# Lightning attention and quantised FFN block: wider DRAM rows for q and k, the first unit's q from fp32 products, another order in the mixed slots

## The reference

```
h    = layernorm(x)
q,k,v = split(h @ w_qkv.T + b_qkv)                # 16 heads of 32
per chunk of 128 tokens, per head, state S (32 x 32), decays lam:
  out = (q * decay_q) @ S + ((q @ k.T) * dmask) @ v
  S   = lam**128 * S + (k * decay_k).T @ v
x    = x + layernorm(out @ w_out.T + b_out)
g    = silu(layernorm(x) @ e4m3(gate_w) * gate_scale)
u    = layernorm(x) @ e4m3(up_w) * up_scale
x    = x + layernorm((g * u) @ e4m3(down_w) * down_scale)
```

## Time and profile before

| | before |
|---|---|
| runs | 988.04 us (987.9 to 988.89, 3 runs) |
| profiled execution | 988.57 us, span 986.8 us |
| TensorE busy | 958.7 us, 97% |
| VectorE busy | 690.4 us, 70% |
| ScalarE busy | 509.1 us, 52% |
| GpSimd busy | 687.6 us, 70% |
| main DMA queue | 296672 packets, 157.86 MB, 67.4% of 16 engines' span |
| DMA packets in all | 297642, of them 141632 under 512 B, 272832 under 2 KB |

### The profile page before, as it was taken

The page is one execution under the profiler, slowest core; times in us unless marked ns, Lnnn a source line. Parts: engine busy times, 40 slices in busy tenths (PEclk is TensorE's granted clock), DMA queues, the critical chain, the costliest instruction groups (busy, mean ns, idle before and its releaser), DMA issues.

```text
span 986.8 us, 22045 instructions
## 1 busy us (share of the span) xinstructions
PE 958.7 (97%) x8498; PEld 708.9 (72%) x8498; DVE 690.4 (70%) x1359; ACT 509.1 (52%) x985; POOL 687.6 (70%) x837
## 2 busy tenths in 40 slices
PE   8999999999998999999999999999999999999996
PEld 6777777786766777767677676767767676776764
DVE  7999998875887675767667576766757676665422
ACT  3656665565654544636354463635446363544522
POOL 2699998986775675849567584947758594775733
PEclk9999999999999999999999999999999999999999
DMA  9899899999983983847658284766828476512200
GB/s 322 210 290 265 255 276 293 277 254 297 229 207 88 202 180 56 196 93 163 131 127 176 61 194 94 163 128 129 191 48 193 92 165 125 127 52 43 41 26 22
DMA packets 297642, 159.88 MB, mean 162 GB/s; under 512 B 141632, under 2 KB 272832, under 8 KB 297408
## 3 DMA queue, kind: packets, MB, share of 16 engines
q1 hardware_dynamic: 296672, 157.86, 67.4%
q10 hardware_dynamic: 864, 0.61, 0.2%
HBM read 82.93 MB, written 41.94 MB: 127 GB/s over the span
## 4 chain that ended last, share of the span: by engine, by line
PE 57%; DVE 17%; POOL 11%; issue 10%; ACT 4%; DMA 1%; POOLq 0%; DVEq 0%; SPq 0%; ACTq 0%
PE bank L892 17%; PE bank L874 12%; PE bank L767 8%; PE att L767 7%; PE bank L782 7%; POOL att_pool L1059 4%; DVE stats L1326 3%; DVE p L1367 3%; DVE state_hl L1397 3%; DVE w_pool L1460 2%; POOL rstd L998 2%; ACT w_pool L596 2%; POOL w_pool L1077 2%; PE att L851 1%; DVE state L1386 1%
## 5 line engine op out<-in xcount | busy, mean ns | idle before, releaser
L874 PE MATMUL bank<-f_pool,gate_q 128*128 128x256 f16 x1536 | 185.0, 274 | 4.3 <-ACT w_pool L596 3.8
L874 PE MATMUL bank<-f_pool,up_q 128*128 128x256 f16 x1536 | 183.7, 273 | 1.5
L892 PE MATMUL bank<-down_q,w_pool 128*128 128x512 f16 x768 | 168.3, 379 | 0.0
L874 PEld LDWEIGHTS bank<-f_pool,gate_q 128*128 128x128 f16 x1536 | 147.4, 98 | 27.0 <-ACT w_pool L596 6.5
L874 PEld LDWEIGHTS bank<-f_pool,up_q 128*128 128x128 f16 x1536 | 149.4, 98 | 22.4 <-DVE w_pool L1460 5.1
L1059 POOL TENSOR_TENSOR att_pool<-p,att_pool 128x512 f16<-128x512 f32 x128 | 145.7, 1159 | 28.0 <-ACT att_pool L548 27.9
L1460 DVE SCALAR_TENSOR_TENSOR w_pool<-bank,us_t,w_pool 128x256 f32<-128x256 f32 x192 | 84.1, 479 | 112.5 <-ACT w_pool L596 54.7
L995 POOL TENSOR_TENSOR rstd<-mv,eps_t 128x1 f32<-128x1 f32 (+1 forms) x112 | 30.1, 269 | 181.3 <-DVE mv L1329 181.3
L892 PEld LDWEIGHTS bank<-down_q,w_pool 128*128 128x128 f16 x768 | 74.0, 98 | 86.9
L1077 POOL TENSOR_TENSOR w_pool<-w_pool 128x512 f16<-128x512 f32 x96 | 111.3, 1165 | 28.0 <-ACT w_pool L602 27.9
L548 ACT CAST att_pool<-p 128x512 f16<-128x512 f32 x128 | 75.7, 615 | 62.4 <-DVE p L1367 62.3
(11 more groups left out here) (145 smaller groups left out, 1826.4 us busy)
## 6 DMA issues: line engine op xcount, KB each, us to landing
xr<-in_x SPq DMA_DIRECT2D x32, 512.0 KB, 4.6
dram_qk<-qk_hl SPq DMA_DIRECT2D x64, 256.0 KB, 3.7
att_pool<-dram_qk SPq DMA_DIRECT2D x64, 256.0 KB, 5.3
f_pool<-dram_qk SPq DMA_DIRECT2D x64, 256.0 KB, 5.6
dram_kd<-kd_hl SPq DMA_DIRECT2D x32, 256.0 KB, 2.9
dram_v<-vv SPq DMA_DIRECT2D x32, 256.0 KB, 3.7
qn_pool<-dram_qk SPq DMA_DIRECT2D x32, 256.0 KB, 6.2
out_x<-w_pool SPq DMA_DIRECT2D x32, 256.0 KB, 2.3
```

Of the source, the lines that this page charges most:

```text
L874: ins = nc.tensor.matmul(b[:, j * TOK:(j + 1) * TOK], w[:, k, o * P:(o + 1) * P], x1_hl[:, v % 2, part, k], start=(k == 0 and part == 0), ...
L892: ins = nc.tensor.matmul((b_gate, b_up)[t][:, :], h_hl[:, part, k, t * P:(t + 1) * P], down_q[:, k], start=(k == 0 and part == 0), stop=(k ...
```

## The change

The change has three parts.

1. **Layout of q and k in DRAM.** Within a unit and half, `dram_qk` is ordered by head dimension, head group and then all 1024 values, for [k][p][t] before. A spill or a q load now moves rows of 2 KB (pattern 4 x 32 x 1024 in DRAM, 128 rows of 1024 in SBUF), for 512 bytes (128 x 4 x 256). A stack loads in rows of 8 KB: three DMAs for k, two for q, for four and four. The heads stand in another order in the stack, and `scores` indexes them so. Decayed k and v keep their layout.
2. **First unit.** x(0) is loaded, normalised and halved tile by tile; TensorE turns its fp32 tiles (`turn_first`), ScalarE copies them out, and q of unit 0 comes from 16 fp32 products with the unsplit weights (`project_first`), scaled when it is evacuated. The weights are split in the order k, v, q, with x(1)'s normalisation behind k's part. The bias maximum is taken of one tile with twelve columns, ahead of the weights; the v bias, and the scales of the FFN, are loaded later. The constant products are 40, 6 and 12. The wout maximum is spread in unit 3 for unit 2.
3. **Mixed slots.** VectorE takes four masked scores earlier, and an `o_max` ahead of a `state_lo`; in slot 2 VectorE's and ScalarE's first FFN steps (`product`, `silu`) go ahead of the attention's.

The diff, cut to its core:

```diff
@@ memory
-        dram_qk = nc.dram_tensor("dram_qk", [units, 2, 2, KT, P, TOK], F16, kind="Internal").ap()
+        dram_qk = nc.dram_tensor("dram_qk", [units, 2, 2, DH, HG, KT * TOK], F16, kind="Internal").ap()
+        x_first = f_magic[0][:, 0:KT * TOK].rearrange("p (k t) -> p k t", k=KT)
@@ SP: spill_q (spill_k alike), load_stack, load_q, load_unit, start
-                    sp.dma_start(dram_qk[n, 0, part].rearrange("k p t -> p k t"), qk_hl[:, part, 0:KT]
+                    sp.dma_start(dram_qk[n, 0, part].rearrange("d j f -> j d f"),
+                                 qk_hl[:, part, 0:KT].rearrange("p k t -> p (k t)")).then_inc(q_spilled, 16)
-                for r in range(4):
-                    sp.dma_start(stacks[s % 2][DH * r:DH * (r + 1), which],
-                                 dram_qk[s, which, parts[r]].rearrange("g (j d) t -> d (g j) t", d=DH)
+                for row, first, last in pieces:
+                    sp.dma_start(stacks[s % 2][DH * row:DH * (row + last - first), which].rearrange("d h t -> d (h t)"),
+                                 dram_qk[s, which, first:last].rearrange("s d j f -> (s d) (j f)")
-                    sp.dma_start(qn[:, s % 2, part], dram_qk[s, 0, part].rearrange("k p t -> p k t")
+                    sp.dma_start(qn[:, s % 2, part].rearrange("p k t -> p (k t)"),
+                                 dram_qk[s, 0, part].rearrange("d j f -> j d f")).then_inc(q_in[s % 2], 16)
-                    load_stack(s, 1, (0, 0, 1, 1))
+                    load_stack(s, 1, ((0, 0, 2), (2, 1, 2), (3, 0, 1)))
-                    load_stack(s, 0, (0, 1, 0, 1))
+                    load_stack(s, 0, ((0, 0, 2), (2, 0, 2)))
-            load_x(0)
+            for t, landed in enumerate((x_first_in, x_in[0])):
+                sp.dma_start(x_src(0)[:, t], x_u[0, :, t]).then_inc(landed, 16)
@@ ScalarE, start
-            x_normalise(0)
-            x_hi(0)
+            x_normalise_tile(0, 0)
+            x_hi_tile(0, 0)
+            x_normalise_tile(0, 1)
+            x_first_tile(0)
+            x_hi_tile(0, 1)
+            x_first_tile(1)
+            act.dma_start(bv[:, :], b_v).then_inc(bv_in, 16)
             act.wait_ge(w_scale_d, 1)
-            for part in range(3):
+            for part in (1, 2, 0):
                 for half in range(2):
                     w_hi(third(wqkv_hi, part, half), third(w_stage, part, half))
-            x_normalise(1)
-            x_hi(1)
+                if part == 1:
+                    x_normalise(1)
+                    x_hi(1)
@@ ScalarE, slot
-                if attends:
+                if s == 2:
+                    silu(v, 0)
                     probs_hi(s, 0, 0)
-                silu(v, 0)
+                else:
+                    if attends:
+                        probs_hi(s, 0, 0)
+                    silu(v, 0)
@@ TensorE
+            def turn_first(t):
+                pe.wait_ge(nrm_d[LN_X], t + 1)
+                for k in range(KT):
+                    ins = nc.tensor.transpose(b_s[t][:, k * P:(k + 1) * P], x_src(0)[:, t, k * P:(k + 1) * P], eye)
+                ins.then_inc(x_first_mm, 1)
+            def project_first(o):
+                for k in range(KT):
+                    ins = nc.tensor.matmul(qk_bank(0, o // 2)[:, o % 2 * TOK:(o % 2 + 1) * TOK],
+                                           w_stage[:, k, o * P:(o + 1) * P], x_first[:, k], start=(k == 0),
+                                           stop=(k == KT - 1))
+                if o % 2:
+                    ins.then_inc(qk_mm, 1)
+                if n == 1 and i == 0:
+                    pe.wait_ge(w_lo_d, 6)
-                    pe.wait_ge(w_lo_d, 6)
+                    pe.wait_ge(w_lo_d, 4)
-                                               stacks[s % 2][:, 1, HG * g + j, c * P:(c + 1) * P],
+                                               stacks[s % 2][:, 1, KT * j + g, c * P:(c + 1) * P],
-                if k == 2:
+                if k == 3:
                     spread_wout_max()
-                project_qk(k, 0)
-                project_qk(k, 1)
+                if k:
+                    project_qk(k, 0)
+                    project_qk(k, 1)
-            for n in range(100):
-                nc.tensor.matmul(b_up[:, 0:2 * P], warm[:, 0:P], warm, start=True, stop=True)
+            constant_products(40)
+            pe.wait_ge(eye_in, 16)
+            turn_first(0)
+            constant_products(6)
+            turn_first(1)
+            constant_products(12)
+            pe.wait_ge(x_first_d, 2)
+            for k in range(KT):
+                pe.wait_ge(w_in[k], 16)
+            project_first(0)
             spread_w_max()
-            for n in range(36):
-                nc.tensor.matmul(b_up[:, 0:2 * P], warm[:, 0:P], warm, start=True, stop=True)
+            project_first(1)
+            project_first(2)
+            project_first(3)
@@ VectorE, start
+                dve.wait_ge(bias_in, 16)
+                link(nc.vector.tensor_reduce(col(7), bqk[:, :], AX.X, ALU.max, apply_absolute_value=True))
+                nc.vector.tensor_scalar(col(4), col(7), 1.0 / 256.0, None, ALU.mult)
                 for k in range(KT):
...
-                    if k == 1:
-                        dve.wait_ge(bias_in, 16 * N_BIAS)
-                        nc.vector.tensor_reduce(col(7), bqk[:, :], AX.X, ALU.max, apply_absolute_value=True)
-                        link(nc.vector.tensor_reduce(col(8), bv[:, :], AX.X, ALU.max, apply_absolute_value=True))
-                        link(nc.vector.tensor_tensor(col(7), col(7), col(8), ALU.max))
-                        nc.vector.tensor_scalar(col(4), col(7), 1.0 / 256.0, None, ALU.mult)
@@ VectorE, first_slot
+                masked(0, 1, 0)
                 k_lo(LEAD, 2)
-                masked(0, 1, 0)
@@ VectorE, second_slot
+                masked(1, 1, 0)
                 k_lo(n, 3)
-                masked(1, 1, 0)
+                masked(1, 1, 1)
                 out_sum(1, 0)
-                masked(1, 1, 1)
                 v_sum(n, 0)
                 carry_and_state(1, 1)
                 v_sum(n, 1)
+                o_max(1, 0)
                 state_lo(1, 1)
-                o_max(1, 0)
...
+                masked(2, 0, 0)
                 o_lo(1)
@@ VectorE, slot
+                if s == 2:
+                    product(v, 0)
                     carry_and_state(s, 0)
-                product(v, 0)
-                if v >= 1:
-                    y2_moments(v - 1, 1)
+                else:
+                    if attends:
+                        masked(s, 0, 0)
+                        carry_and_state(s, 0)
+                    product(v, 0)
+                    if v >= 1:
+                        y2_moments(v - 1, 1)
```

More of the change, by code:

```diff
@@ L506, in q_hi @@
                     ins = nc.scalar.activation(q32[:, i, j], qk_bank(n, i)[:, j * TOK:(j + 1) * TOK],
-                                               ACT.Identity, bias=bqk[:, o:o + 1])
+                                               ACT.Identity, bias=bqk[:, o:o + 1],
+                                               scale=1.0 if n else small[:, 11:12])
                 ins.then_inc(q_d, 1)
@@ L747, in spread_wout_max, with constant_products @@
                 ins.then_inc(wout_max_all, 1)
+            def constant_products(count):
+                for n in range(count):
+                    nc.tensor.matmul(b_up[:, 0:2 * P], warm[:, 0:P], warm, start=True, stop=True)
+            def turn_first(t):
[10 more added lines that the diff above has]
+                    ins.then_inc(qk_mm, 1)
             def project_qk(n, i):
-                if i == 0:
+                if i == 0 or n == 0 and i == 2:
                     pe.wait_ge(*x_landed(n))
+                if n == 1 and i == 0:
+                    pe.wait_ge(w_lo_d, 6)
                 if n < LEAD:
@@ L763, in project_qk @@
                     for k in range(KT):
[L764 to L765 removed]
+                        if n == 0 and i == 2 and j == 0 and k % 2 == 0:
+                            pe.wait_ge(w_lo_d, k // 2 + 1)
                         for q, (a, b) in enumerate(((0, 0), (0, 1), (1, 0))):
@@ L1089, in _ @@
             pool.wait_ge(eps_d, 3)
-            inverse_std_x(0)
+            for t in range(T):
+                inverse_std_first(t)
             x_lo(0)
@@ L1233, in prepare_qkv @@
                 dve.wait_ge(w_scale_d, 1)
-                nc.vector.tensor_scalar(bqk[:, :], bqk[:, :], col(11), None, ALU.mult)
+                link(nc.vector.tensor_scalar(bqk[:, :], bqk[:, :], col(11), None, ALU.mult))
+                for n, part in enumerate((1, 2, 0)):
+                    for half in range(2):
+                        w_lo(2 * n + half, third(wqkv_lo, part, half), third(wqkv_hi, part, half),
+                             third(w_stage, part, half))
+                dve.wait_ge(bv_in, 16)
                 link(nc.vector.tensor_scalar(bv[:, :], bv[:, :], col(11), None, ALU.mult))
-                for part in range(3):
```

(9 more changed lines are left out.)

59 lines of the change are left out of this document (36 added, 23 removed).

## The result

The change takes 1097.52 us in the median (1092.92 to 1099.15, 5 runs), the kernel before 988.04 us (5 runs of the same chip): a ratio of 1.1098, 95% interval 1.1081 to 1.1115, slower by 11%. The forecast was 984.1 us; rival D, on the slower side, had a chance of 0.22 and a middle of 1020.

What follows compares the result with a forecast made beforehand. TensorE's own work was taken to bound the projections and steady slots, leaving the start and mixed slots to win: 988.57 − 3.9 (start) − 0.4 (first slot) + 0.4 (second slot and slot 2), less 0.53, is 984.1 us; range 978 to 988.5.

Steps and rivals of the forecast that it cites:

- rival D: Spills of q and k run on four of sixteen DMA engines: 15 to 64 us more, middle 1020; chance 0.22.
- Layout of q and k: Wider DRAM rows for spills, q loads and stacks: same bytes, TensorE not waiting there, so 0 gained if spread like the others.
- second estimate: Rival D's other bytes priced by today's busy time, 11.1 us per engine; slower once fewer than eight engines are used.
- Start: First unit: TensorE alone 5.5 to 7.3 us earlier, of which 3.9 us kept; ends 2.5 and 7.3.
- The 2 us kept for a lower clock: First fp32 products of unit 0: 2 us extra if their first 4 us run at the lower clock after TensorE's idle time.
- unit 2's moments: VectorE reaches them between 28.9 and 30.7, for 29.97 before; taken as 0.5 us earlier.
- the smallest of the bounds: Start's gain limited to 3.9 us by x(3), against 5.7 by the k evacuation and 7.3 by TensorE.
- x(3): Its transposes land at 66.4, TensorE wants it at 69.8: slack 3.4, with VectorE's 0.5 a gain of at most 3.9 us.
- the k evacuation: VectorE's last one of unit 0, needed for unit 1's k: slack 5.2, with the 0.5 a gain of at most 5.7 us.
- First slot: A masked score ahead of a k evacuation starts its probabilities up to 1.6 us earlier: −0.4 us, ends 0 and −1.6.
- Second slot and slot 2: TensorE up to 4.4 us early mid-slot 2, given back by the end because GpSimd is full: +0.4, ends −4.4 and +1.4.
- The clock's part: Slot 2: the half-clock stretch behind the first gate product (5.33 us for 3.49) goes, 1.8 us.

Runs made afterwards that it cites:

- layout_only: The kernel before with the change's DRAM layout of q and k alone (spills 4x32x1024, stack loads in 8-KB rows): 1085.62 us, ratio 1.0989.
- slots_only: The kernel before with only the new order in the first slot, the second slot and slot 2: 990.27 us, ratio 1.0023.
- k_only4: The change with q as 128 contiguous rows of 2 KB and only k still spilled as 4x32x1024: 1039.99 us (median of three), ratio 1.0501.
- turn_first4: The change with x(k+2)'s transposes put ahead of the q and k spills on the SP queue: 1125.25 us, ratio 1.1388.
- turn_early: `rows2k_start` with x(1)'s two transposes ahead of two of three FFN weight pieces and the output weights on the SP queue: 985.09 us, ratio 0.9974.
- rows2k_start: The kernel before with q and k as 128 contiguous rows of 2 KB and the new start, mixed slots as before: 985.92 us, ratio 0.9982.

## Why the prediction was wrong

**Layout of q and k: the step that failed.** It was costed at 0 ("Bounded by rows: 0 if it spreads like the others") and measured +97.5 us alone. The forecast took the value of the nearest rows, all of which begin with 128 or 32, and gave the other case 0.22. In the runs the spills do not spread like the others: they move 102 GB/s, a quarter of the best 415 of before, and 128 rows of the same 2 KB bring the loss to nothing. The row that could have weighed more was known: the queue was 93% busy in a unit, so that a spill on a quarter of the engines could hardly be hidden. The Trainium skill's page "DMA: Bandwidth & Descriptors" has the row that the prediction cites ("Rules for kernel authors": at most as many engines as the outermost dimension), and in "Why a DMA increments its semaphore by 16 and not by 1" it says how many: the largest number up to 16 that divides the outermost dimensions (other than 1) of both patterns. By that rule 4, 2 and 32 give 4, 2 and 16; the traces agree with 102, 51 and up to 490 GB/s.

**Rival D's price.** That four engines run was right, the price (15 to 64 us more, middle 1020) too small. Its period, 17.5 to 21.2 us, held: 20.4. The price multiplied the excess by 13 plain units and took 8 us off. Missing were the units that also load stacks (periods up to 28.0 us), the first two slots, whose stacks and spills come as late (+18.9 and +10.2), and 7.6 at the end, of which `layout_only` has 1.2 and `slots_only` 2.3. Two of its figures are slightly off: by its second estimate it decides below nine engines (8.9), not eight, and to take in all of D the range had to be seven times as wide, not five. That the period held is in part luck. By the same sum of work `k_only4` should have had 13.9 us and no loss, and it took 18.0. By the periods of the four layouts the cause is less the engines' total work, as the rival had it, than a chain: the spill of one unit must land before the next unit's halves are written, and the transposes hold the SP queue meanwhile. `turn_first4` bears out the first link; how the two share the loss stays open.

**Start.** TensorE's side in the change:

```profile
12.42 1.97 PE L789 MATMUL bank<-f_pool,att_pool 128*128 128x256 f32 x8 [1.94 <-DMA att_pool<-in_w_qkv_t]
14.31 0.49 PE L765 MATMUL bank<-state,small 128*128 128x128 f32 x2
14.64 5.34 PE L789 MATMUL bank<-f_pool,att_pool 128*128 128x256 f32 x24
19.82 5.57 PE L815 MATMUL att<-o_t,w_pool 128*128 128x256 f16 x48
25.64 5.35 PE L830 MATMUL bank<-w_pool,o_t 128*128 128x512 f16 x24 [0.25 <-DVE w_pool L1307]
32.16 5.41 PE L815 MATMUL bank<-xr,w_pool 128*128 128x256 f16 x48 [1.17 <-DMA xr<-hl]
37.41 5.40 PE L815 MATMUL att<-xr,w_pool 128*128 128x256 f16 x48
42.65 5.34 PE L830 MATMUL bank<-w_pool,xr 128*128 128x512 f16 x24
```

12 fp32 products in 5.34 us are 0.45 each, as worked out; all 16 were done at 20, and v began at 25.64. The 2 us kept for a lower clock rested on a wrong reading: the spread took 0.49 us here too (14.31), without idle time ahead of it and at a granted clock of 1.00, and before the clock was 1.00 from 16 to 17 us as well. The idea itself was sound for a longer wait, as `turn_early` shows. The last low half ended at 27.97 (28.0 forecast), and unit 2's moments began at 28.80, earlier than the 29.5 forecast, since the two tiny operations took 0.16 us each.

What failed is "the smallest of the bounds", on both sides. x(1) was not on the list: its transposes, moved 6.6 us earlier, ran into the loads issued ahead of them. And x(3), whose slack was to allow 3.9, did not bind: in `rows2k_start` its transposes start at 56.9 and 58.3, for 58.3 and 61.1 before, and TensorE takes it at 64.55 without a wait, 5.9 us early. There the gain was 5.7 at unit 3 and 5.0 at unit 13, inside the 2.5 to 7.3 but above 3.9. What shows as a wait is the k evacuation (0.40 and 0.29 us), whose bound was 5.7. Nor was it seen that the gain takes the room of the later transfers; with narrow rows the start lost 7 us.

**First slot:** −0.4 forecast; in the profiled execution of `slots_only` it is 21.15 us for 21.39, −0.2.

**Second slot and slot 2:** +0.4 forecast, some +2.3 measured. The clock's part was right (the slow stretch behind the first gate product went), and so was that GpSimd, full, sets the end. What was mis-sized is how late GpSimd gets h's first piece, "about 1 us": it was 1.9 us (2.1 from unit 15's v), because ScalarE makes its high half behind the state's, which now waits 2.49 us for VectorE. All of it is left at the slot's end, and what TensorE gained ahead turns into the wait of 2.31 us.

## What to carry to other kernels

Look at the outermost dimension of both sides of every DMA before its row size: here 2-KB rows with a 4 in front moved 102 GB/s, 512-byte rows with 128 in front about 346. Where a buffer is reused every unit, the total work of the DMA engines is not enough to price a slow spill, because the next unit's writes wait for it to land: half the slow bytes, 5.1 us of them, still cost 2.3 us per unit in `k_only4`. And when a start is made earlier, list every input of the next unit with the queue it stands in, and check that the busiest transfers further on can bear the lost slack.

## What was not expected of the hardware

Two transposes queued behind spills of four engines took 11.93 us of the SP queue, for some 3 us before, about as long as the stretch of 102 GB/s beside them. Two transposes issued behind 3.9 MB of loads took 9.88 us for 3.29. An issue of a 64-KB spill took the SP queue about 0.5 us (8 in 3.69 and in 4.69 us), as much as one of 256 KB (2 in 0.92 before). And after waits of 3.06 and 5.4 us TensorE ran at a granted clock of 0.50 (48 products in 6.89 for 5.40 us), after one of 1.94 it did not.
